# Delta rule: the key blocks' transfers on ScalarE, the inverse's on the sync engine

## The reference

```python
def step(S, inputs):
    q_t, k_t, v_t, g_t, b_t = inputs
    S = S * jnp.exp(g_t)[..., None, None]
    kv = jnp.einsum('bhk,bhkv->bhv', k_t, S)
    u = b_t[..., None] * (v_t - kv)
    S = S + jnp.einsum('bhk,bhv->bhkv', k_t, u)
    o_t = jnp.einsum('bhk,bhkv->bhv', q_t * scale, S)
    return (S, o_t)
```

## Time and profile before

| | us |
|---|---|
| median of 3 runs | 2786.35 |
| lowest, highest | 2782.04, 2786.99 |
| the profiled execution | 2785.99 |
| its span | 2784.2 |

### The profile page before, as it was taken

The page is one execution under the profiler, slowest core; times in us unless marked ns, Lnnn a source line. Parts: engine busy times, 40 slices in busy tenths (PEclk is TensorE's granted clock), DMA queues, the critical chain, the costliest instruction groups (busy, mean ns, idle before and its releaser), DMA issues. The chain is left out here.

```text
span 2784.2 us, 34289 instructions
## 1 busy us (share of the span) xinstructions
PE 2625.1 (94%) x12650; PEld 1959.8 (70%) x12650; DVE 1635.9 (59%) x2428; ACT 882.6 (32%) x1342; POOL 387.8 (14%) x676
## 2 busy tenths in 40 slices
PE   8965888789999999999999989999999989999998
PEld 7854787678888888888888864333333678888887
DVE  6873777664445444554455377777776465645554
ACT  3343444231111111112111125666665322222221
POOL 0027877400000000000000021222210100000000
PEclk9987999889999999999999998999999999999999
DMA  2342332210000000000000014222221001100001
GB/s 92 103 135 46 76 90 45 54 49 24 23 23 23 23 23 23 23 23 23 23 23 23 0 48 73 73 71 72 73 79 35 31 16 37 40 31 15 15 16 46
DMA packets 104219, 122.32 MB, mean 44 GB/s; under 512 B 47455, under 2 KB 80479, under 8 KB 102439
## 3 DMA queue, kind: packets, MB, share of 16 engines
q1 hardware_dynamic: 104102, 120.79, 15.2%
HBM read 88.26 MB, written 24.64 MB: 41 GB/s over the span
## 5 line engine op out<-in xcount | busy, mean ns | idle before, releaser
L2256 DVE TENSOR_REDUCE att_top<-att_scores 128x1 f32<-128x1024 f32 x256 | 312.3, 1224 | 128.5 <-PE att_scores L2416 128.2
L296 DVE TENSOR_TENSOR fp_hidden<-fp_gelu,fp_up 128x512 f32<-128x512 f32 x128 | 88.1, 688 | 440.8 <-PE fp_up L75 377.9
L2129 ACT ACTIVATE att_probs<-att_scores 128x1024 f32<-128x1024 f32 x256 | 262.1, 1024 | 189.9 <-PE att_scores L2441 188.0
L2456 PE MATMUL att_out<-att_probs,att_padded 128*64 128x512 f32 x1024 | 269.1, 615 | 3.0 <-issue 2.8
L278 DVE TENSOR_TENSOR k_stream<-k_stream,fp_down 128x512 f32<-128x512 f32 x256 | 175.4, 686 | 84.0 <-PE fp_down L75 80.6
L356 ACT ACTIVATE fp_gelu<-fp_gate 128x512 f32<-128x512 f32 x128 | 76.3, 596 | 420.0 <-PE fp_gate L75 419.2
L73 PE MATMUL fp_gate<-fp_feat_hi,fp_w_hi 128*128 128x512 f32 x512 | 200.9, 392 | 3.8 <-DVE fp_feat_lo L266 3.8
L74 PE MATMUL fp_gate<-fp_feat_lo,fp_w_hi 128*128 128x512 f32 x512 | 200.3, 391 | 0.0
L75 PE MATMUL fp_gate<-fp_feat_hi,fp_w_lo 128*128 128x512 f32 x512 | 200.1, 391 | 0.0
L73 PE MATMUL fp_down<-fp_w_hi,fp_h_hi 128*128 128x512 f32 x512 | 199.5, 390 | 0.0
L75 PE MATMUL fp_up<-fp_feat_hi,fp_w_lo 128*128 128x512 f32 x512 | 199.5, 390 | 0.0
(11 more groups left out here) (337 smaller groups left out, 5560.2 us busy)
## 6 DMA issues: line engine op xcount, KB each, us to landing
f_early<-codes SPq DMA_DIRECT2D x16, 768.0 KB
f_early<-scales SPq DMA_DIRECT2D x16, 768.0 KB
att_stacks<-rotated SPq DMA_DIRECT2D x96, 128.0 KB
la_values<-w_sparse SPq DMA_DIRECT2D x10, 1024.0 KB, 4.8
f_early<-qkv SPq DMA_DIRECT2D x14, 576.0 KB, 5.9
att_stacks<-rotated SPq DMA_DIRECT2D x96, 64.0 KB
k_stream<-hidden SPq DMA_DIRECT2D x16, 256.0 KB, 4.8
att_stacks<-att_rot_hi SPq DMA_DIRECT2D x64, 64.0 KB
```

The source lines that it names most:

```text
L296: dve.tensor_tensor(hidden[:, c, :], gelu[:, c, :], up_ps[c][:], ALU.mult).then_inc(product_done, 1)
L2129: act.activation(probs[:, tile % PROBS, :], key_bank(tile)[:], ACT.Exp).then_inc(exp_done, 1)
L2256: dve.tensor_reduce(top[g % 2][:, STACK + t:STACK + t + 1], query_bank(tile)[:], AX.XY, ALU.max, negate=True).then_inc(max_done, 1)
L2456: last = pe.matmul(out[rows, :], padded[:, g % 2, t, :], probs[:, t, half * TB:(half + 1) * TB], start=t == 0, stop=t == T - 1)
```

## The change

The functions `take_blocks` and `place_blocks` are given the engine that issues them. The sync engine still calls them for chunks 0 and 1. For the chunks 2 to 7 ScalarE calls them, in pass c for chunk c + 2: the take behind `copy_queries`, the placing behind `square_outputs`. The sync engine's `blocks_of_chunks` becomes `inverse_of_chunk`, with the transfers of the inverse alone. The waits inside the functions are the same as before.

```diff
+        def take_blocks(engine, c):
+            engine.wait_ge(a_done, BH * (c + 1))
+            if c:
+                engine.wait_ge(l_in, 16 * c)
...
+        def place_blocks(engine, c):
+            if c >= 2:
+                engine.wait_ge(base_done, c - 1)
+            engine.wait_ge(l_out, 16 * QUARTERS * (c + 1))
...
-            def blocks_of_chunks(given, taken):
+            def inverse_of_chunk(given):
                 if given == 0:
                     sp.wait_ge(zero_done, 3)
-                if taken is not None:
-                    take_blocks(taken)
                 take_inverse(given, base_t, base_done, blocks_t, t_out, diag_in)
-                if taken is not None:
-                    place_blocks(taken)
                 place_inverse(given, blocks_t, t_out, diag, m_ps, diag_in)
...
                 if c + 1 < CHUNKS:
-                    blocks_of_chunks(c + 1, c + 2 if c + 2 < CHUNKS else None)
+                    inverse_of_chunk(c + 1)
...
                 if ahead:
                     copy_queries(ahead)
+                    take_blocks(act, ahead)
                 if c != LAST:
                     square_outputs(c)
+                if ahead:
+                    place_blocks(act, ahead)
+                if c != LAST:
                     turn_blocks(c + 1)
```

More of the change, by code:

```diff
@@ L942, in delta_rule @@
         STEPS = 2 * (BASE - 1)
+        def take_blocks(engine, c):
+            engine.wait_ge(a_done, BH * (c + 1))
+            if c:
+                engine.wait_ge(l_in, 16 * c)
+            for q in range(QUARTERS):
+                at = slice(BASE * q, BASE * (q + 1))
+                engine.dma_start(blocks_l[q].rearrange("i s t -> s i t"), a_t[at, c % 2, :, at]).then_inc(l_out, 16)
+        def place_blocks(engine, c):
+            if c >= 2:
+                engine.wait_ge(base_done, c - 1)
+            engine.wait_ge(l_out, 16 * QUARTERS * (c + 1))
+            engine.dma_start(base_l[base_rows(c), :, :], blocks_l.rearrange("q i s t -> (q i) s t")).then_inc(l_in, 16)
         @block.sync
@@ L953, in start_base @@
                              eye.partition_broadcast(NB)).then_inc(t_init[c % 2], 16)
[L955 to L967, removed]
             def take_inverse(c, base, produced, scratch, out, done):
@@ L1013, in _ @@
             sp.dma_start(w32, w_out.rearrange("(k p) n -> p k n", p=P)).then_inc(arrived, 16)
-            take_blocks(0)
-            place_blocks(0)
+            take_blocks(sp, 0)
+            place_blocks(sp, 0)
             sp.wait_ge(kq_ps, PAIRS_OF_KEYS)
             load(2)
-            take_blocks(1)
-            place_blocks(1)
-            blocks_of_chunks(0, None)
+            take_blocks(sp, 1)
+            place_blocks(sp, 1)
+            inverse_of_chunk(0)
             for c in range(CHUNKS):
```

## The result

The changed kernel takes 2794.83 us (median of 8 runs, 2791.49 to 2797.93). In the same comparison the kernel before takes 2786.18 us (8 runs, 2782.04 to 2788.07). The ratio is 1.0034, its 95% interval 1.0025 to 1.0044: **8.65 us slower**. The profiled execution took 2796.49 us with a span of 2794.7, against 2785.99 and 2784.2 before.

What follows compares the result with a forecast made beforehand. A two-chunk loop through placing, GpSimd's inverse and TensorE was taken as the bound. Later placings in passes 0, 2 and 5 delay chunk 7 by 5.8 us: 2785.99 + 5.8 = 2791.8 us, range 2786.5 to 2797.

Steps and rivals of the forecast that it cites:

- What bounds the kernel: Delta rule: a two-chunk loop through placing, GpSimd's inverse and TensorE, 82.6 us; GpSimd alone needs 41 to 42 per chunk.
- D(c): Time at which TensorE's products with the diagonal blocks of chunk c start; for chunk 7 forecast 530.55, against 524.71.
- What the change removes: Sync engine's queue: only pass 0 gains, its inverse went 2.6 us late; chunk 1 comes 1.3 us earlier, then lost.
- The placing's new place: ScalarE, pass at 351: the placing is issued at the second square's end, 355.74, 2.9 us later than before.
- ScalarE's sequencer runs ahead of its datapath: Bound on the three chained placings: each would leave 0.4 us earlier, minus 1.2 us.
- The price of an issue: ScalarE's four take issues: the sync engine's 1.87 us; bounds per issue nearly nothing and about double 0.47 us.
- rival C: A ScalarE issue costs 0.8 us or more, or waits for the datapath; landing becomes last: 2795.5 us, chance 0.2.
- The sum: Placings chained in passes 0, 2 and 5 delay chunk 7's products from 524.71 to 530.55: plus 5.8 us, 2791.8.
- F(2) - D(2): Pass 2, from the start of the diagonal-block products to the end of the second square_outputs: 37.9 us.
- Rival A: ScalarE's issues nearly free, placing leaves at the second square's dispatch, landings short: not measurably slower, 2788 us, chance 0.3.
- Rival B: ScalarE places at once, GpSimd's gap shrinks some 1 us in each of three links: faster, 2782.5 us, chance 0.06.
- The signs I named: Changed profile: placing within 0.5 us of second square's end, GpSimd's first wait about 9.5 us, alternating waits, chunk 7 near 530.

Runs made afterwards that it cites:

- lateness alone, on the sync engine: The kernel before, all transfers on the sync engine, but the placing waits until both squares are done: 2793.74 us, ratio 1.0029.
- half as many filling products: The changed kernel with 18, 16 and 23 unused products filling TensorE's waits before chunks 2, 4 and 6: 2796.52 us, ratio 1.0040 against the kernel before.
- the early version: The changed kernel with ScalarE's take ahead of copy_queries and its placing right behind it, ahead of both squares: 2788.11 us, ratio 1.0010 against the kernel before.

## Why the prediction was right or wrong

I forecast 2791.8 us from a profiled execution of 2785.99, that is, plus 5.8. It became plus 8.65 by the medians and plus 8.5 in the stage that was summed. The mechanism and its direction were right, the size was a third too small.

- **What bounds the kernel.** Right. The two-chunk loop from D(c) over the placing, GpSimd's inverse and back to D(c+2) carries the loss, and lateness alone, on the sync engine, gives the same pattern and most of the size.
- **What the change removes.** Right that only pass 0 gains: the sync engine sent the inverse at 266.66 there, as soon as it was ready (269.77 before), and TensorE didn't wait for it. Right too that it is lost again one pass later.
- **The placing's new place.** Right about what holds it, the second square. It left at its dispatch (358.33 and 358.39), not at its end, so the bound "ScalarE's sequencer runs ahead of its datapath" came true in this pass: 0.4 us earlier than in my sum. In passes 0, 4 and 5 it was held by another thing, below.
- **The price of an issue.** Half right. I took the sync engine's 1.87 us for the four, and in passes 1, 2 and 3 ScalarE needed 1.88. In the other three passes they took far longer. ScalarE's timeline in pass 4:

```profile
441.03 0.31 ACTq L950 DMA_DIRECT2D blocks_l<-f_weight  x1
...
441.37 3.03 ACTq L950 DMA_DIRECT2D blocks_l<-f_weight  x3
444.53 0.90 ACT L1416 ACTIVATE dr_square<-dr_bank 128x384 f32<-128x384 f32 x2 [2.97 <-issue]
446.80 0.32 ACTq L956 DMA_DIRECT2D f_blocks<-blocks_l  x1
```

and the sync engine's:

```profile
442.39 2.47 SPq L981 DMA_DIRECT2D dr_diag<-blocks_t  x4
```

  3.37 us on ScalarE (441.03 to 444.40), 2.47 on the sync engine. Here the squares are ready and wait for the issuing, and the placing waits for the landing: its lag is 8.4 us. Company isn't the whole reason. In pass 2 the two engines issued at the same time too (ScalarE from 354.43 to 356.31, the sync engine as in the first row below), and nothing got longer. In pass 5 the last three of ScalarE's four took 2.41 us instead of 1.54 (the second row), while the sync engine issued nothing between 455.7 and 487.1:

```profile
355.00 1.90 SPq L981 DMA_DIRECT2D dr_diag<-blocks_t  x4
```

```profile
481.89 2.41 ACTq L950 DMA_DIRECT2D blocks_l<-f_weight  x3
```

  The longer issues delay the landing: the take's last piece landed at 273.26, 446.73 and 485.81 in passes 0, 4 and 5, and the placing left 0.1 us later each time. This is what rival C described, an issue that costs ScalarE 0.8 us or more and a landing that becomes the last thing: 0.81 and 0.84 each in passes 0 and 4, 0.69 in pass 5, 0.47 in the others. Rival C's time, 2795.5, is nearer to the result than my forecast. Page "DMA: Bandwidth & Descriptors" of the Trainium skill, section "Issuing engines are not separate DMA queues", says that issuing on several engines concurrently saves only the sequencer's time. In passes 0 and 4 the trace shows less than that: the issuing itself was longer on both engines (3.23 and 3.37 us against 1.88, 2.35 and 2.47 against 1.85).
- **The sum.** D(2), D(3) and D(4) came at 319.58, 360.18 and 406.00, forecast 320.65, 360.05 and 405.95; D(0) stood 0.84 earlier, which I hadn't assumed, so measured from D(0) these are 0.2 early, 1.0 late and 0.9 late. D(5) to D(7) came at 446.97, 493.19 and 532.35, with 445.35 for D(5) and 530.55 for D(7) forecast. From D(0) to D(7) I forecast 293.35 us and 295.99 passed, 2.6 more. **The terms that were too small:** F(2) - D(2), forecast 37.9, took 39.24 (358.82 - 319.58), in which TensorE was busy 6.0 us of the 7 behind 324.6, where it had been busy all 7 before. D(4) to D(5), forecast 39.4, took 40.97: the 24 products at clock 0.50 took 5.49 us against the 4.43 of the pass I had read it from. F(5) - D(5), forecast 37.5 "TensorE has not idled now", took 485.94 - 446.97 = 38.97. These are 1.3, 1.6 and 1.5 us, 4.4 in all. **Too large** was the way from F to GpSimd's start, forecast 3.4, measured 2.51 (361.33 - 358.82) and 2.75 (488.69 - 485.94), 1.5 us in all; and the rest, from there to D(4) and D(7), came to about nothing (0.7 more, 0.6 less). With D(2) 0.2 early, 4.4 less 1.5 less 0.2 is 2.7, the 2.6 that was missing but for rounding. This adds up one execution against one execution; how far each term would stay in another isn't known.
- **What I had left out** is a third loop, from one pass's squares to the next's. In pass 1 D came 2.0 us earlier than before (274.06 against 276.04), yet the last key product only 0.4. VectorE's rows, first of the kernel before and then of the changed one:

```profile
306.37 0.60 DVE L1585 SCALAR_TENSOR_TENSOR dr_att<-dr_bank,dr_weight,dr_att 128x128 f32<-128x128 f32 x2
```

```profile
305.94 0.60 DVE L1585 SCALAR_TENSOR_TENSOR dr_att<-dr_bank,dr_weight,dr_att 128x128 f32<-128x128 f32 x2
```

  The second square's end is 40.2 us apart between passes 0 and 1 of the kernel before, and 40.3 in the changed one (272.70 to 313.03), whatever D does. In the changed kernel this distance is 40.3, 45.8, 41.4, 45.2 and 40.5 us: it never falls below 40.3 there, nor below 40.2 before. So a pass in which the blocks come early doesn't make good what a late one costs, and F - D is longer in it, which fits the 1.5 us of F(5) - D(5). It also is the likely reason why less lag than before gains nothing. I read it from these spacings; no experiment took this loop apart. The 40.2 is no fixed floor: the distance was down to 39.8 us in the kernel with the late placing on the sync engine, and to 39.7 with half as many filling products. Nor is it shown which engine closes the loop. From its start on the products of one chunk until it is free for the next, TensorE took 38.9 to 39.6 us in passes 1 to 5 of the kernel before and 39.8 to 41.5 in the changed one, and 1.0 to 2.5 us of the latter it waited for VectorE's `dr_z` (0.7 to 1.8 before).
- **Rival A** (not slower in any measurable way) fell: the loss is 0.34%, its interval 0.25 to 0.44%. Two of its reasons held, the early dispatch (in passes 1 to 3) and short landings (2.94 and 2.81 us from the issue at 358.39 and 485.88 to GpSimd), but its price left out the passes that got longer.
- **Rival B** (faster) fell as argued: the placing is behind both squares. And even where the placing is not, in the early version or at once on the sync engine, nothing is won.
- **The signs I named** mostly showed: first wait 9.67 (about 9.5), the others alternating between 1.6 and 9.9, none of TensorE's before odd chunks, 4.3 to 6.4 before even ones (I said 5 to 7), chunk 7 at 532.35 (near 530). The placing started within 0.5 us of the second square's end in four passes, and 0.6 and 1.4 us behind it in passes 0 and 4. One sign of being wrong showed as well: an issue on ScalarE had another size than 0.47 us in three of six passes.

## What to carry to other kernels

A DMA given to a compute engine leaves when that engine's queue comes to it: before moving one, measure from the moment its data is complete to the moment its neighbours in the new queue are done, and compare with the old queue; here 2.6 us more of it on a loop without slack, with the issuing, cost 8.65 us in six passes. A late transfer in a loop of period two showed up here as alternating waits, long and none, and the passes that came early gave nothing back; that a second loop with the same period is why was read from spacings alone. When only half of a chained pair is moved to another queue, look at what stands behind the half that stays: it now waits for the other engine.

## What the hardware showed that I had not expected

- ScalarE's sequencer issues a DMA while its datapath is still working: the first take of pass 2 left at 354.43, 0.34 us into the first of two copies of 0.48 us and 0.04 before the second one started, which stands ahead of it in the list; the placing left 0.06 us after the start of a square of 0.49 us.
- The price of an issue isn't fixed. Four on ScalarE took 1.88 us in three passes of the changed kernel and 3.23, 3.37 and 2.75 in the others; four on the sync engine took 1.85 us, and 2.24, 2.62 and 2.80 at three places of the kernel before, where no other engine issues. Counted from 230 to 620 us in all fourteen traces, four issues in a row of one line took over 2.0 us on ScalarE in 19 of 26 cases in which the sync engine issued at the same time and in 6 of 22 in which it didn't; on the sync engine in 9 of 20 beside ScalarE and in 32 of 232 alone. So company makes it much more frequent, and isn't its only cause; what is stays open.
- The transfers that ScalarE issues have a DMA queue of their own in the profile (q10, 9984 packets).
- Filling TensorE's wait kept the clock at its higher level and shortened the products from 5.49 to 2.95 us, and the time of the kernel showed no gain: 2784.96 against 2785.49 us, ratio 0.9998 (0.9989 to 1.0007).
